# A preparing stage taken out of a perceiver kernel: its keys and values become column groups of the first cross attention, and its norm moves into the masked attention

## The reference

```python
# cross attention of layer 0: 16 heads of 64
kv = context @ w_kv; k, v = jnp.split(kv, 2, axis=-1)
attn = softmax(einsum(q, k) * scale); out = einsum(attn, v)

# cross attention of layer 1: 8 heads of 64, masked, over the normed context
xn = layernorm(x, ln_x_g, ln_x_b)          # x is the context here
kv = jnp.concatenate([xn, ln], axis=1) @ Wkv

# cross attention of layer 2: linear attention, needs only sums over the context
kh = _layernorm(k @ wk, ln_gamma, ln_beta); vh = _layernorm(v @ wv, ln_gamma, ln_beta)
k_prime = (relu(kh) + EPS_K) * em;  vh = vh * em
kv = einsum('bhnd,bhne->bhde', k_prime, vh);  z needs k_prime.sum
```

## Time and profile before

| | |
|---|---|
| median of 3 runs (lowest, highest) | 3282.53 us (3282.21, 3284.53) |
| the profiled execution, its own time | 3287.21 us |
| its span, first to last instruction | 3285.6 us |
| PE, PEld busy | 2809.3 us (86%), 2244.3 us (68%) |
| DVE, ACT, POOL busy | 1830.1 us (56%), 1530.2 us (47%), 475.2 us (14%) |
| mean granted TensorE clock | 0.927 |

### The profile page before, as it was taken

The page is one execution under the profiler, slowest core; times in us unless marked ns, Lnnn a source line. Parts: engine busy times, 40 slices in busy tenths (PEclk is TensorE's granted clock), DMA queues, the critical chain, the costliest instruction groups (busy, mean ns, idle before and its releaser), DMA issues. The chain is left out here.

```text
span 3285.6 us, 72653 instructions
## 1 busy us (share of the span) xinstructions
PE 2809.3 (86%) x26026; PEld 2244.3 (68%) x26026; DVE 1830.1 (56%) x5010; ACT 1530.2 (47%) x3126; POOL 475.2 (14%) x915
## 2 busy tenths in 40 slices
PE   6788699999999999995666999999767559999973
PEld 5666588888888888884345888888546446777752
DVE  7999455555555555554574555555453347565625
ACT  5777455555555555552443555555300002444441
POOL 3333111111111111100012222222000011000000
PEclk9999899999999999997787999999869687999985
DMA  3334311111111111001442111110124264334210
GB/s 112 119 119 118 114 57 42 39 36 35 35 35 35 35 35 35 29 2 36 163 156 86 35 35 35 35 35 22 55 110 166 107 248 128 123 114 125 75 35 18
DMA packets 128243, 244.15 MB, mean 74 GB/s; under 512 B 16448, under 2 KB 89168, under 8 KB 122576
## 3 DMA queue, kind: packets, MB, share of 16 engines
q1 hardware_dynamic: 95696, 208.26, 18.9%
q10 hardware_dynamic: 28672, 19.27, 1.9%
q0 software_dynamic: 3584, 12.58, 1.2%
HBM read 201.27 MB, written 38.80 MB: 73 GB/s over the span
## 5 line engine op out<-in xcount | busy, mean ns | idle before, releaser
L340 PE MATMUL l0x_psum<-l0x_fast 128*128 128x448 f32 x1344 | 331.6, 383 | 20.3 <-DVE l0x_fast L545 12.8
L470 ACT ACTIVATE l0x_sbuf<-l0x_sbuf 128x896 f32<-128x896 f32 x224 | 233.2, 1041 | 231.2 <-DVE l0x_sbuf L565 231.2
L1447 DVE CUSTOM_DVE_ANT_0 l3x_sbuf<-l3x_psum,l3x_fast,l3x_sbuf 128x896 f32<-128x896 f32 x224 | 253.4, 1150 | 140.0 <-PE l3x_psum L1294 135.6
L1378 ACT ACTIVATE l3x_sbuf<-l3x_psum 128x512 f32<-128x512 f32 x392 | 213.7, 596 | 220.7 <-PE l3x_psum L1313 220.2
L355 PE MATMUL l0x_psum<-l0x_fast 128*128 128x512 f32 x1176 | 310.5, 401 | 0.9 <-POOL l0x_fast L625 0.9
L551 DVE TENSOR_TENSOR l0x_fast<-l0x_psum,l0x_fast 128x448 fp32r<-128x448 f32 x224 | 140.0, 625 | 298.3 <-ACT l0x_fast L450 298.3
L340 PEld LDWEIGHTS l0x_psum<-l0x_fast 128*128 128x128 f32 x1344 | 237.2, 190 | 41.8 <-issue 12.9
L565 DVE CUSTOM_DVE_ANT_0 l0x_sbuf<-l0x_psum,l0x_sbuf 128x896 f32<-128x896 f32 x224 | 248.9, 1149 | 25.6 <-PE l0x_psum L369 25.6
L186 PE MATMUL prep_psum<-prep_sbuf 128*128 128x256 f32 x784 | 196.8, 395 | 70.0 <-DMA prep_sbuf<-in_ctxT 63.8
L576 DVE COPY l0x_sbuf<-l0x_psum 128x384 f32<-128x384 f32 x224 | 124.8, 557 | 236.3 <-PE l0x_psum L386 236.3
L355 PEld LDWEIGHTS l0x_psum<-l0x_fast 128*128 128x128 f32 x1176 | 213.5, 188 | 57.3 <-issue 16.7
(11 more groups left out here) (700 smaller groups left out, 5625.7 us busy)
## 6 DMA issues: line engine op xcount, KB each, us to landing
l3x_fast<-ctx_high SPq DMA_DIRECT2D x112, 224.0 KB, 3.7
l1f_sbuf<-in_L_ffn_W SPq DMA_DIRECT2D x16, 1024.0 KB, 6.8
l2f_sbuf<-in_L_ffn_W SPq DMA_DIRECT2D x16, 1024.0 KB, 6.9
prep_sbuf<-in_ctx_rows SPq DMA_DIRECT2D x98, 128.0 KB, 2.1
prep_sbuf<-in_ctxT SPq DMA_DIRECT2D x98, 128.0 KB, 2.5
xnT<-prep_sbuf ACTq DMA_DIRECT2D x98, 128.0 KB, 2.3
l0x_sbuf<-in_ctxT SPq DMA_DIRECT2D x14, 896.0 KB, 6.2
ctx_high<-l0x_fast SPq DMA_DIRECT2D x14, 896.0 KB, 7.8
```

Of the source, the lines that this page charges most:

```text
L340: mm = pe.matmul(ps[:, 0:width], self.wk[w][:, c, pr * T:(pr + 1) * T], x[:, c, lo:lo + width], start=(j == 0), stop=(j == len(products) - 1))
L470: act.activation(self.p[:, (2 * m + a) % 4, 0:width], self.sm[:, a, 0:width], ACT.Exp, scale=-1.0, bias=self.negm[:, n % 2, 2 * pr + a:2 * ...
L1378: act.activation(p[:, u % 4, :, :, :].rearrange("p h a t -> p (h a t)"), ps_t[slot["tiles", u]][:, :], ACT.Exp).then_inc(s.sem("p"), 1)
L1447: dve.tensor_tensor_reduce(junk[:, a, :].rearrange("p (i c) -> p i c", i=2), ps_s[a][:, :, 0:HALF], bias[:, n * CH:(n + 1) * CH].bitcast(F ...
```

## The change

`stage_prepare` is gone, with `xnT`. Its work is placed thus:

- A new class `ContextSide` rides in `l0x`. Its weights have 512 columns (256 of keys, 256 of values of layer 2) and are split high and low; each context tile becomes one more column group of six products, two in each of the first three steps of a chunk and one in the fourth. ACT copies it out. DVE takes moments in steps 0 to 3, computes the scales in step 4, normalises keys and values in step 5. POOL applies gain, shift and the positive part to the keys after step 5. PE adds the chunk's sum (14 products of 128x130) at the end of step 7, and DVE adds it to a running total. Moments of the raw rows go out as `ctx_mean` and `ctx_rstd`.
- The value buffer is now 512 columns wide and turns over every four steps instead of every chunk, so that there is room; the first chunk's 14 value groups are no longer done ahead of the first step.
- `l1x` reads the raw transposed context, with mean and reciprocal deviation broadcast to all partitions, and norms each chunk itself: six instructions over 896 columns on POOL (`pool_norm`), two chunks ahead, at the second step of each chunk. For the first chunk DVE does half.

```diff
+        if side is not None:
+            for n in range(NCH):
+                for t in range(CT):
+                    self.plan.setdefault(P * n + t // 2, []).append(("side", n * CT + t, 0))
...
+            sums = [("sum", m // P, 0)] if side is not None and self.closes(m) else []
+            uses += keys[:1] + groups[:1] + keys[1:] + groups[1:] + turns + sums
...
     def pe(self, pe):
...
                 self.pe_turn(pe, m - 2)
+            if self.side is not None and self.closes(m):
+                self.side.pe_sum(pe, m // self.P, self.pe_slot(pe, "sum", m // self.P, 0))
...
     def dve(self, dve):
...
                 self.dve_keys(dve, m + 1, 0)
+            if self.side is not None and m > 0 and self.closes(m - 1):
+                n = (m - 1) // self.P
+                self.side.dve_summed(dve, n, self.ps_kv[self.slot["sum", n, 0]])
...
                 self.dve_acc(dve, m - 2)
+            if self.side is not None and m < self.M:
+                self.side.dve_step(dve, *divmod(m, self.P))
...
+    def norm_part(self, eng, n, c):
+        s = self.s
+        eng.wait_ge(s.sem("raw_in"), (n + 1) * 16)
+        eng.wait_ge(s.sem("mean_in"), (n + 1) * 16)
+        eng.wait_ge(s.sem("rstd_in"), (n + 1) * 16)
+        eng.wait_ge(s.sem("gain_in"), 32)
+        part = self.raw[:, c, :]
+        eng.tensor_tensor(part, part, self.mean[:, :], ALU.subtract).then_inc(s.sem(f"centered{c}"), 1)
+        eng.wait_ge(s.sem(f"centered{c}"), n + 1)
+        eng.tensor_tensor(part, part, self.rstd[:, :], ALU.mult).then_inc(s.sem(f"scaled{c}"), 1)
+        eng.wait_ge(s.sem(f"scaled{c}"), n + 1)
+        eng.tensor_scalar(part, part, self.gain[:, 0, c:c + 1], self.gain[:, 1, c:c + 1], ALU.mult, ALU.add).then_inc(s.sem("normed"), 1)
...
     def pool(self, pool):
...
+            if pr == 1 and self.norm_dram is not None and n + 2 < NCH:
+                self.pool_norm(pool, n + 2)
+            if self.side is not None:
+                self.side.pool_step(pool, n, pr)
...
+    def dve_step(self, dve, n, pr):
+        if pr < 4:
+            for t in range(2 * pr, min(2 * pr + 2, CT)):
+                self.dve_moments(dve, n, t)
+        elif pr == 4:
+            self.dve_scales(dve, n)
+        elif pr == 5:
+            self.dve_normal(dve, n)
...
+    def dve_moments(self, dve, n, t):
...
+        dve.bn_stats(self.st[:, t, 0, :], self.k(t)).then_inc(s.sem("side_st"), 1)
+        dve.bn_stats(self.st[:, t, 1, :], self.v(t)).then_inc(s.sem("side_st"), 1)
+        dve.bn_stats(self.st[:, t, 2, :], self.rows[:, t, :]).then_inc(s.sem("side_seen"), 1)
...
+    def dve_scales(self, dve, n):
...
+        for t in range(CT):
+            for i in range(3):
+                dve.bn_aggr(self.mv[:, t, i, :], self.st[:, t, i, :]).then_inc(s.sem("side_mv"), 1)
...
+        link(dve.tensor_tensor(var, self.mv[:, :, :, 1], self.eps[:, :, :], ALU.add))
+        link(dve.tensor_scalar(half.bitcast(I32), var.bitcast(I32), 1, None, ALU.logical_shift_right))
+        link(dve.tensor_scalar(r.bitcast(I32), half.bitcast(I32), -1.0, 1597463007.0, ALU.mult, ALU.add))
+        for _ in range(3):
+            link(dve.scalar_tensor_tensor(out=half, in0=r, scalar=-0.5, in1=r, op0=ALU.mult, op1=ALU.mult))
+            link(dve.tensor_tensor(half, half, var, ALU.mult))
+            link(dve.scalar_tensor_tensor(out=r, in0=half, scalar=1.5, in1=r, op0=ALU.add, op1=ALU.mult))
...
+    def dve_normal(self, dve, n):
...
+        for t in range(CT):
+            ins = dve.tensor_scalar(self.k(t), self.k(t), self.mv[:, t, 0, 0:1], self.r[:, t, 0:1], ALU.subtract, ALU.mult)
+        ins.then_inc(s.sem("side_z"), 1)
+        for t in range(CT):
+            ins = dve.tensor_scalar(self.v(t), self.v(t), self.mv[:, t, 1, 0:1], self.scale[:, t:t + 1], ALU.subtract, ALU.mult)
+        ins.then_inc(s.sem("side_v"), 1)
...
+    def pool_step(self, pool, n, pr):
...
+        if pr == 5:
...
+            pool.wait_ge(s.sem("side_z"), n + 1)
+            pool.tensor_tensor(k, k, gain, ALU.mult).then_inc(s.sem("side_gained"), 1)
+            pool.wait_ge(s.sem("side_gained"), n + 1)
+            pool.tensor_tensor(k, k, shift, ALU.add).then_inc(s.sem("side_shifted"), 1)
+            pool.wait_ge(s.sem("side_shifted"), n + 1)
+            pool.tensor_scalar(k, k, 0.0, 1e-6, ALU.max, ALU.add).then_inc(s.sem("side_k"), 1)
```

More of the change, by code:

```diff
@@ L323, in pe_slot @@
                 pe.wait_ge(self.s.sem("v"), i + 1)
+            elif kind == "side":
+                pe.wait_ge(self.s.sem("side"), i + 1)
+            elif kind == "sum":
+                pe.wait_ge(self.s.sem("summed"), i + 1)
             else:
@@ L342, in pe_keys, with pe_group @@
         mm.then_inc(s.sem("k_ps"), 1)
-    def pe_group(self, pe, g):
+    def pe_group(self, pe, use):
         s = self.s
-        n, t, e = self.groups[g]
-        ps = self.pe_slot(pe, "v", g, 0)
+        if use[0] == "v":
+            n, t, e = self.groups[use[1]]
+            weights, done = [w[:, :, e * 512:(e + 1) * 512] for w in self.wv], s.sem("v_ps")
+        else:
+            n, t = divmod(use[1], CT)
+            weights, done = [w[:, :, :] for w in self.side.w], s.sem("side_ps")
+        ps = self.pe_slot(pe, *use)
         if n < NCH:
@@ L393, in pe_values @@
         pe.wait_ge(s.sem("pTb"), self.tb_count(2 * m + 3 if m + 1 < self.M else 2 * m + 2))
-        pe.wait_ge(s.sem("v"), max(g for g, (c, _, _) in enumerate(self.groups) if c == n) + 1)
+        pe.wait_ge(s.sem("v"), self.ready[m // 4])
         self.wait(pe, "outT", m)
@@ L410, in pe @@
         pe.wait_ge(s.sem("q_low"), 1)
-        pe.wait_ge(s.sem("w_low"), 2)
+        pe.wait_ge(s.sem("w_low"), 2 if self.side is None else 3)
         for i in range(2):
             self.pe_keys(pe, 0, i)
-        for g in self.plan[-1]:
-            self.pe_group(pe, g)
         for m in range(self.M + 2):
@@ L493, in act_prepare @@
                            scale=self.scale).then_inc(s.sem("q_high"), 1)
-        for name, (high, _), raw in (("wk", self.wk, self.wk_raw), ("wv", self.wv, self.wv_raw)):
+        weights = [("wk", self.wk, self.wk_raw), ("wv", self.wv, self.wv_raw)]
+        if self.side is not None:
+            weights.append(("side", self.side.w, self.side_raw))
+        for name, (high, _), raw in weights:
             act.wait_ge(s.sem(name + "_in"), 16)
@@ L542, in dve_prepare @@
         dve.sem_inc(s.sem("q_low"), 1)
-        for i, ((high, low), raw) in enumerate(((self.wk, self.wk_raw), (self.wv, self.wv_raw))):
+        weights = [(self.wk, self.wk_raw), (self.wv, self.wv_raw)]
+        if self.side is not None:
+            weights.append((self.side.w, self.side_raw))
+        for i, ((high, low), raw) in enumerate(weights):
             dve.wait_ge(s.sem("w_high"), i + 1)
@@ L728, in _ @@
         def _(sp):
+            pa.sp_raw(sp, 0)
             pa.sp_weights(sp)
+            side.sp_small(sp)
             pa.sp(sp)
```

458 lines of the change are left out of this document (209 added, 249 removed).

## The result

The changed kernel takes 3512.95 us (median of four runs, 3507.21 to 3519.47), the kernel before 3283.53 in the same series. The ratio is 1.0697, 95% interval 1.0675 to 1.0719: slower by 229 us. The direction was forecast, but 3384 was said, and the range ended at 3480. The changed kernel's profiled execution spans 3509.9 us, against 3285.6.

What follows compares the result with a forecast made beforehand. The prediction took DVE to bound the preparing stage and PE the first cross attention. Removing 344.35 us and adding 381.5 + 3 in `l0x` and 61 in `l1x` gave +101 us: 3384 us, range 3265 to 3480.

Steps and rivals of the forecast that it cites:

- moments: `l0x`, steps 0 to 2: six moments at 0.34 us take 2.05, 0.35 too long, so 1.1 us in three steps.
- scales: `l0x`, step 4: 21 aggregates, 12 chained operations and 3 more on DVE take 4.8 us, making PE wait 3.1.
- normalising, PE's wait for the keys: `l0x`, after step 5: DVE's normalising block delays the next keys, so PE waits 2.9 us a chunk.
- POOL ahead of alpha: `l0x`, step 7: ACT's alpha waits for `diff` behind POOL's side-key work, costing PE 4.4 us a chunk.
- running total: `l0x`, after the chunk's sum: PE's next group waits 1.85 us until DVE, behind the first keys, takes the total.
- low clock: `l0x`: one of three waits a chunk brings PE's 1.2 GHz level, losing 1.5 us (bounds 0 and 4.5).
- costing of step 5: `l0x`: 14 DVE operations with per-partition scalars, priced like L133 (0.41 us long, 0.33 apart): 4.6 us, wait 2.9.
- third rival: `l0x`: POOL's first product shuts out DVE's seven value normalisations, adding 4.03 us a chunk, +56, 3440 us; chance 0.07.
- POOL's (max, add): `l0x`: POOL's last side-key instruction over 1792 elements takes 1.9 or 6.5 us; the slow figure was taken.
- chain behind it: `l1x`: load 7.5 us, POOL's norm 10.8, then late `diff` and alpha: PE waits 3.6 us in twelve chunks, 43.
- fourth rival: `l0x` and `l1x`: the waits do not reach PE; without any, -158 us, 3124 us; chance 0.15.
- break-even: `l0x`: the change breaks even at 20.0 us a chunk; with PE work 12.4, waits must stay under 7.6.

Runs made afterwards that it cites:

- e1: Changed kernel with DVE normalising the seven value tiles before the seven key tiles, so POOL starts after DVE's normalising: 3431.57 us, ratio 1.0447.
- e2: Changed kernel without POOL's three instructions on the side keys (gain, shift, positive part), values still behind keys on DVE: 3316.79 us, ratio 1.01.
- e7: Changed kernel with DVE's value instruction also writing a sum of each row that nothing reads; order and POOL unchanged: 3383.02 us, ratio 1.0304.
- e4: Changed kernel with POOL's last instruction on the side keys as (mult, add) in place of (max, add), positive part left out: 3463.4 us, ratio 1.0548.
- e3: Changed kernel with POOL's norm in `l1x` split in two halves, at the second and third steps of a chunk: 3435.98 us, ratio 1.046.
- e6: e5 with DVE's side work in two places of a step and the running total taken before the next keys: 3162.68 us, ratio 0.9628.
- e5: Changed kernel with values first on DVE, the `l1x` norm split, and POOL's third side-key instruction one step later: 3250.06 us, ratio 0.9899.
- e8: Changed kernel with DVE taking the running total before, not behind, the subtraction of the next keys: 3507.62 us, ratio 1.0676.

## Why the prediction was wrong

The terms of the sum for a chunk of `l0x`, against the trace of the changed kernel. The measured waits are idle times ahead of PE's lines; the PE work and the clock are what remains of each step's lengthening over the same step before. A chunk went from 80.91 us (the L340 rows at 563.08 and 1372.13 of the trace before lie ten chunks apart) to 116.06 (the L379 rows at 476.01 and 1520.51 of the trace after lie nine apart), that is 35.15 where 27.25 were forecast:

| term | forecast | measured |
|---|---|---|
| seven groups | 9.3 | 9.95 |
| sum of the chunk | 3.1 | 3.12 |
| moments | 1.1 | 0 |
| scales | 3.1 | 2.33 |
| normalising, PE's wait for the keys | 2.9 | 16.12 |
| POOL ahead of alpha | 4.4 | 0 |
| running total | 1.85 | 1.62 |
| low clock | 1.5 | 2.0 |

**The step that failed** is the costing of step 5, "14 operations with per-partition scalars like L133 (0.41 long, 0.33 apart): 4.6, wait 2.9". It priced each instruction by a row where nothing ran on POOL, while the change itself puts POOL's 14.5 us beside the second seven. The two failing terms are coupled. Together they were forecast at 7.3 and measured at 16.1: 8.8 us a chunk, 123 us over fourteen, where the forecast missed by 129 in all. The other terms of a chunk came out 0.9 us smaller together, and `l1x` 22 us larger. POOL's wait did not show because DVE kept PE longer still, so that POOL's work ended behind the same wait and added nothing to it; e1 brought it out at 5.5.

**The third rival had the mechanism, with a wrong price and a wrong reading.** It said that values would be held "until POOL's first product is through, 4.03 us". It was right that one is held, but when a POOL instruction ends only that held one gets through, and the next is caught by POOL's next instruction. The hold is three of POOL's instructions long: PE's wait grew by 13.6 us (16.12, against 2.52 in e2), not by 4.03. And the text gave it 7%, "Against it: L133's 0.41 us is one plain pass with one SBUF input", and said that by the Trainium skill's rule the form "would not be held". e7 shows the opposite: this form is held, and the one with an accumulator isn't. The rule was not what failed, but the reading of the form as a plain pass; the text left the other reading open and priced it at 4.03 us. The trace of before had a case that wasn't read. A TENSOR_SCALAR in the preparing stage (128x3, with numbers in place of pointers), with a median of 131 ns, starts twice while POOL's instruction L1030 runs; it takes 0.55 and 0.50 us there and ends with it. The first of the two:

```profile
44.52 0.64 POOL L1030 TENSOR_TENSOR prep_sbuf<-prep_sbuf 128x256 f32<-128x256 f32 x1
44.63 0.55 DVE L982 TENSOR_SCALAR prep_sbuf<-prep_sbuf 128x3 f32<-128x3 f32 x1
```

**POOL's (max, add)** was taken at 6.5 from two rows; it is 6.29, and 1.75 with (mult, add) in e4, where 1.9 was said. **The chain behind it** in `l1x` came as forecast: the norm's load 8 us after its issue (7.5 said), the six instructions 10.9 (10.8), a wait of 4.1 a chunk (3.6), 49 us in all (43). Too small was the clock: 9 us, where about 29 went, 2.4 in each of twelve chunks (what e3 gained in the stage, 76.4 us, less the 47.7 of waits that went). With the 5 that are left for the stage's start (9 said), `l1x` is 83 and not 61.

**The fourth rival**, that waits don't reach PE, is refuted for the kernel as changed. Its arithmetic stands as a limit: without waits it gave 3124, and e6, which takes most of them away, is at 3163. **The break-even** of 20.0 us a chunk was also near: with `l1x` at +83 it is 18.5. e5 has 21.5 a chunk (102.41 less 80.91) and `l1x` mended, so that the break-even is some 24 there, and it is faster; the changed kernel has 35.15, and is slower.

## What to carry to other kernels

Before DVE work is put beside GpSimd work, look for rows of that very DVE form with and without a long POOL instruction beside it, and price the first; an order in which DVE is done before it releases POOL avoids the hold, at the price that POOL starts later (in e1 by the 2.3 us of the values). A lightly loaded engine is not free if something small that others need stands in its queue: cut its work to pieces that fit between two of those small instructions, and look again, since a removed wait uncovers the next one. Here moving instructions turned a loss of 7% into a gain of 3.7%.

## What was not expected of the hardware

- A held DVE instruction ends just behind the POOL instruction, and the next DVE instruction is held by POOL's next: 4.20, 4.18 and 6.45 us, for POOL's 4.20, 4.03 and 6.29.
- A duration does not tell whether a form can be held. The held form takes 410 ns for 256 columns. A TENSOR_SCALAR with a number in place of the pointers takes about that for 512, as the groups of the changed kernel show, so that the pointer form looks slow and plain:

```profile
L2425 DVE TENSOR_SCALAR l0f_sbuf<-l0f_sbuf 128x512 f32<-128x512 f32 x16 | 6.0, 420 | 0.0
```

- The pair of functions sets POOL's speed: 3.5 ns a column for (max, add), 1.0 for (mult, add), both over 1792 float32 columns.
- Waits of 2.34 and 2.33 us at the same place of the program, in the changed kernel and in e8, were followed by 2.4 GHz in the one and by 1.2 GHz in the other.
